# Cross attention: row sums by GpSimd, a scaled head output, and output products that accumulate over 14 heads

## The reference, cut to what matters

```python
q = (inputs_q @ Wq).reshape(b, sq, H, HD) * (1.0 / np.sqrt(HD))
k = (inputs_kv @ Wk).reshape(b, skv, H, HD)
v = (inputs_kv @ Wv).reshape(b, skv, H, HD)
scores = jnp.einsum('bqhd,bkhd->bhqk', q, k)
attn = jax.nn.softmax(scores, axis=-1)
ctx = jnp.einsum('bhqk,bkhd->bqhd', attn, v).reshape(b, sq, H * HD)
return ctx @ Wo
```

## Time and profile before

| | us |
|---|---|
| median of 3 runs | 1637.68 (1637.64 to 1637.73) |
| the profiled execution | 1636.64 |
| its span | 1634.4 |
| PE busy | 1607.9 |
| DVE busy | 1093.6 |
| ACT busy | 703.9 |
| POOL busy | 167.9 |

### The profile page before, as it was taken

One profiled execution on the slowest core, in us unless ns is written; L12 is line 12 of the kernel. 1 busy time (PEld: TensorE's weight loads), 2 busy tenths in 40 slices (PEclk: granted clock), 3 DMA queues, 4 the chain that ended last, 5 costly groups with the idle time before them and its releaser, 6 DMA issues.

```text
span 1634.4 us, 22632 instructions
## 1 busy us (share of the span) xinstructions
PE 1607.9 (98%) x8766; PEld 1258.1 (77%) x8766; DVE 1093.6 (67%) x1742; ACT 703.9 (43%) x941; POOL 167.9 (10%) x233
## 2 busy tenths in 40 slices
PE   9999999999999999999999999999999999999998
PEld 8887888888888888888888888887857757544544
DVE  4445787777778778777777779999583762633333
ACT  4334454454445454444444445655341361322221
POOL 0001000000100000010000001111100072011110
PEclk9999999999999999999999999999999999999999
DMA  7876655554565555465454454334320517489994
GB/s 238 228 228 188 161 134 158 151 145 122 172 163 142 149 142 154 118 185 142 113 139 126 133 136 123 93 102 135 137 92 39 206 52 304 183 255 418 421 425 174
DMA packets 125513, 282.93 MB, mean 173 GB/s; under 512 B 7712, under 2 KB 83680, under 8 KB 119264
## 3 DMA queue, kind: packets, MB, share of 16 engines
q1 hardware_dynamic: 103104, 200.75, 38.7%
q0 software_dynamic: 22304, 80.75, 16.4%
HBM read 206.99 MB, written 74.48 MB: 172 GB/s over the span
## 4 chain that ended last, share of the span: by engine, by line
PE 83%; DVE 8%; DMA 3%; issue 3%; ACT 2%; POOL 0%; SPq 0%; DVEq 0%; ACTq 0%; POOLq 0%
PE bank L478 19%; PE bank L41 19%; PE bank L448 17%; PE bank L500 6%; PE bank L2172 5%; PE bank L499 3%; PE bank L2211 2%; PE bank L1738 2%; PE bank L2197 2%; PE bank L1752 1%; PE bank L526 1%; DVE S L830 1%; PE bank L2201 1%; DVE e_parts L851 1%; PE bank L2157 1%
## 5 line engine op out<-in xcount | busy, mean ns | idle before, releaser
L478 PE MATMUL bank<-wv_parts,cT_hi 128*128 128x512 f32 x1024 | 333.7, 389 | 1.5 <-DMA wv_parts<-wv_dram 1.4
L478 PEld LDWEIGHTS bank<-wv_parts,cT_hi 128*128 128x128 f32 x1024 | 192.2, 188 | 41.8 <-DMA wv_parts<-wv_dram 1.8
L851 DVE TENSOR_TENSOR e_parts<-S,e_parts 128x1024 fp32r<-128x1024 f32 (+1 forms) x129 | 156.8, 1215 | 84.7 <-ACT e_parts L656 82.6
L448 PE MATMUL bank<-cT_hi,wk_hi 128*128 128x512 f32 x512 | 204.6, 400 | 0.0
L647 ACT ACTIVATE S<-S 128x1024 f32<-128x1024 f32 (+1 forms) x129 | 135.9, 1053 | 152.7 <-DVE S L830 152.2
L448 PE MATMUL bank<-cT_lo,wk_hi 128*128 128x512 f32 x512 | 199.8, 390 | 0.0
L448 PE MATMUL bank<-cT_hi,wk_lo 128*128 128x512 f32 x512 | 199.7, 390 | 0.0
L478 PE MATMUL bank<-wv_parts,cT_lo 128*128 128x512 f32 x512 | 199.3, 389 | 0.0
L656 ACT CAST e_parts<-S 128x1024 fp32r<-128x1024 f32 (+1 forms) x129 | 134.8, 1045 | 135.1 <-PE bank L500 128.9
L843 DVE TENSOR_TENSOR esum<-esum,S 128x512 f32<-128x512 f32 x210 | 145.0, 691 | 71.7 <-ACT S L647 68.1
L803 DVE TENSOR_TENSOR mx<-mx,S 128x512 f32<-128x512 f32 x222 | 152.9, 689 | 12.8 <-ACT S L641 9.0
(11 more groups left out here) (300 smaller groups left out, 2661.9 us busy)
## 6 DMA issues: line engine op xcount, KB each, us to landing
w<-in_w_moe SPq DMA_DIRECT2D x32, 2304.0 KB, 14.0
v_dram<-v_out SPq DMA_DIRECT2D x112, 512.0 KB, 4.9
v_back<-v_dram POOLq DMA_DIRECT2D x110, 512.0 KB
ctx_nat<-in_ctx SPq DMA_DIRECT2D x8, 1024.0 KB, 5.1
ctx_raw<-in_ctxT SPq DMA_DIRECT2D x7, 1024.0 KB, 8.5
v_dram<-v_back SPq DMA_DIRECT2D x14, 512.0 KB, 4.8
v_late<-v_dram POOLq DMA_DIRECT2D x14, 512.0 KB
wv_parts<-wv_dram POOLq DMA_DIRECT2D x6, 1024.0 KB, 8.3
```

Source lines behind the costliest of these rows:

```text
L448: t = e.matmul(banks[b][:], l, r, start=(c == 0 and m == 0), stop=(c == DT - 1 and m == 2))
L478: t = e.matmul(banks[b][:], l, r, start=(c == 0 and m == 0), stop=(c == DT - 1 and m == 2))
L851: e.tensor_tensor(lo, S[:, of_chunk(j, m), :], hi.bitcast(F32), ALU.subtract).then_inc(e_split, 1)
```

## The change

For heads 0 to 13 (SUMMED = 14) GpSimd adds the partial sums over partitions with an all-reduce (`add_sums`), VectorE inverts the 256 sums on all partitions (`invert_row`) and multiplies oT by them (`scale_o`), and the output products of these heads accumulate in PSUM banks 5 and 4 without leaving them; `add_heads` adds the two banks to x once. Heads 14 and 15 are finished as before. Since bank 4 is taken, the query projections use the value banks. finish_head moves to chunk 4 (NCH // 2), project_q to chunk 7, after the last scores, and the loads of wq and wo change their waits.

```diff
+        SUMMED = XH - 2
+        def q_bank(h):
+            return banks[FIRST_Q_BANK if h < 2 else V_BANKS[0] if h < LATE + 2 else V_BANKS[1]]
...
             def project_q(h):
-                if h >= 3:
-                    e.wait_ge(x_added, TT * (h - 2))
-                matmuls(e, banks[Q_BANK][:, 0:T], ...
+                if h >= 2:
+                    e.wait_ge(v_split, units(h - 2, NCH - 1)[0] if h < LATE + 2 else QUADS * KVT)
+                matmuls(e, q_bank(h)[:, 0:T], ...
...
             def project_k(h, j):
                 elif n:
                     e.wait_ge(v_split, QUADS * KVT)
+                    e.wait_ge(q_split, h + 1)
...
             def project_v(u):
+                if g and kt % NCH == 0:
+                    e.wait_ge(q_split, HPQ * (g - 1) + kt // NCH + 2)
...
             def weigh(h, j):
                 if j == 0 and h:
-                    e.wait_ge(sum_inverted, h)
+                    e.wait_ge(o_moved, h)
+                    if h > SUMMED:
+                        e.wait_ge(scaled, h)
...
             def finish_head(h):
                 e.wait_ge(o_moved, h + 1)
-                if h < XH - 1:
+                if h == SUMMED:
                     columns_of_sums(h, slice(0, P))
+                if h >= SUMMED:
+                    e.wait_ge(x_added, TT * (h - SUMMED + 1))
+                else:
+                    e.wait_ge(scaled, h + 1)
                 e.wait_ge(wqo_in, qo_value["wo", h])
-                if h:
-                    e.wait_ge(x_added, TT * h)
-                e.wait_ge(q_split, min(h + 3, XH))
                 for i in range(TT):
-                    t = e.matmul(banks[Y_BANKS[i]][:], ..., start=True, stop=True)
+                    t = e.matmul(banks[Y_BANKS[i]][:], ...,
+                                 start=(h == 0 or h >= SUMMED), stop=(h >= SUMMED - 1))
...
TensorE, heads 0 to 11 (in the late loop alike)
-                    if j == 0 and h and starts_quad(h):
-                        finish_head(h - 1)
                     for u in units(h, j):
                         project_v(u)
                     scores(h + 1, j)
-                    if j == 0 and h and not starts_quad(h):
+                    if j == NCH // 2 and h:
                         finish_head(h - 1)
-                    if j == NCH // 2:
+                    if j == NCH - 1:
                         project_q(h + 2)
...
VectorE
+            def invert_row(h):
+                e.wait_ge(sum_ready, h + 1)
+                own.done(e.reciprocal(mxr[:], mxr[:]))
+            def scale_o(h):
+                own.wait(e)
+                e.wait_ge(o_moved, h + 1)
+                e.tensor_tensor(oT[:], oT[:], mxr[:], ALU.mult).then_inc(scaled, 1)
+            def add_heads():
+                e.wait_ge(y_projected, SUMMED)
+                for i in range(TT):
+                    e.tensor_tensor(x[:, i, :], banks[Y_BANKS[i]][:], x[:, i, :], ALU.add).then_inc(x_added, 1)
...
heads 1 to 11: invert_sum(h - 1) in chunk 0 and add_head(h - 1) in chunk 1 go, and after the next shift
+                    if j == 2 and h:
+                        invert_row(h - 1)
+                    if j == 3 and h:
+                        scale_o(h - 1)
heads 12 to 14: the same two go, and after split_k(h + 1, j + 1)
+                    if j == 2:
+                        invert_row(h - 1)
+                        scale_o(h - 1)
+                    if j == 5 and h == XH - 2:
+                        add_heads()
...
GpSimd, in chunk 0 behind largest_score(h)
+            def add_sums(h):
+                e.wait_ge(sum_folded, h + 1)
+                e.wait_ge(max_ready, h + 2)
+                e.partition_all_reduce(mxr[:], esum_t[:], P, bass.bass_isa.ReduceOp.add).then_inc(sum_ready, 1)
...
SyncE
+ wo of head h - 1 is loaded in chunk 0 (after q_projected >= h + 2), wq of head h + 2 in chunk 5
+ (after y_projected >= h); before, both were loaded in turn in chunks 1 and 5
```

More of the change, by code:

```diff
@@ L393, in sync_cross @@
                     load_wk(1)
-            loads = 2
             for h in range(XH):
                 for j in range(NCH):
[L397 to L401, removed]
                     if j == 0:
@@ L405, in sync_cross @@
                             e.wait_ge(*v_spilled(KVT - 1))
-                            load_qo(loads)
-                            loads += 1
+                            load_qo(qo_order.index(("wq", 2)))
+                        elif h < XH - 1:
+                            e.wait_ge(q_projected, h + 2)
+                            load_qo(qo_order.index(("wo", h - 1)))
                         if not has_halves(h):
                             load_wk(h + 2)
[L410 to L413, removed]
+                    if j == 1 and h == XH - 1:
+                        e.wait_ge(y_projected, h)
+                        load_qo(qo_order.index(("wo", h)))
                     if j == NCH - 2 and has_halves(h):
@@ L417, in sync_cross @@
                         spill(u)
+                    if j == 5 and 0 < h < XH - 1:
+                        e.wait_ge(y_projected, h)
+                        load_qo(qo_order.index(("wq", h + 2) if h + 2 < XH else ("wo", h)))
                     if half_at(h, j) is not None:
@@ L429, in project_q @@
                     e.wait_ge(q_split, h)
-                if h >= 3:
-                    e.wait_ge(x_added, TT * (h - 2))
-                matmuls(e, banks[Q_BANK][:, 0:T], [(wq_raw[:, c, :], xT[:, c, :]) for c in range(DT)]).then_inc(q_projected, 1)
+                if h >= 2:
+                    e.wait_ge(v_split, units(h - 2, NCH - 1)[0] if h < LATE + 2 else QUADS * KVT)
+                matmuls(e, q_bank(h)[:, 0:T], [(wq_raw[:, c, :], xT[:, c, :]) for c in range(DT)]).then_inc(q_projected, 1)
             def project_k(h, j):
@@ L518, in finish_head @@
                 e.wait_ge(o_moved, h + 1)
-                if h < XH - 1:
+                if h == SUMMED:
                     columns_of_sums(h, slice(0, P))
+                if h >= SUMMED:
+                    e.wait_ge(x_added, TT * (h - SUMMED + 1))
+                else:
+                    e.wait_ge(scaled, h + 1)
                 e.wait_ge(wqo_in, qo_value["wo", h])
-                if h:
-                    e.wait_ge(x_added, TT * h)
-                e.wait_ge(q_split, min(h + 3, XH))
                 for i in range(TT):
-                    t = e.matmul(banks[Y_BANKS[i]][:], oT[:, i * P:(i + 1) * P], wqo_raw[:], start=True, stop=True)
+                    t = e.matmul(banks[Y_BANKS[i]][:], oT[:, i * P:(i + 1) * P], wqo_raw[:],
+                                 start=(h == 0 or h >= SUMMED), stop=(h >= SUMMED - 1))
                 t.then_inc(y_projected, 1)
@@ L570, in tensor_cross @@
                     scores(h + 1, j)
-                    if j == 0:
+                    if j == NCH // 2:
                         finish_head(h - 1)
-                    if j == NCH // 2 and h + 2 < XH:
+                    if j == NCH - 1 and h + 2 < XH:
                         project_q(h + 2)
@@ L607, in round_q @@
                     e.wait_ge(scored, NCH * h)
-                e.activation(q_hi[:], banks[Q_BANK][:, 0:T], ACT.Copy, scale=Q_SCALE).then_inc(q_rounded, 1)
+                e.activation(q_hi[:], q_bank(h)[:, 0:T], ACT.Copy, scale=Q_SCALE).then_inc(q_rounded, 1)
             def round_ctx(j):
@@ L775, in split_q @@
                 e.wait_ge(q_rounded, h + 1)
-                e.scalar_tensor_tensor(q_lo[:], banks[Q_BANK][:, 0:T], Q_SCALE, q_hi[:].bitcast(F32),
+                e.scalar_tensor_tensor(q_lo[:], q_bank(h)[:, 0:T], Q_SCALE, q_hi[:].bitcast(F32),
                                        ALU.mult, ALU.subtract).then_inc(q_split, 1)
@@ L870, in fold_sum @@
                 e.tensor_reduce(esum_t[:], esum[:].rearrange("p a t -> p t a"), AX.X, ALU.add).then_inc(sum_folded, 1)
+            def invert_row(h):
[5 more added lines that the diff above has]
+                e.tensor_tensor(oT[:], oT[:], mxr[:], ALU.mult).then_inc(scaled, 1)
             def invert_sum(h):
                 e.wait_ge(sum_ready, h + 1)
-                if h:
-                    e.wait_ge(x_added, TT * h)
-                e.reciprocal(small[:, 0:TT], banks[O_BANK][:, T:T + TT]).then_inc(sum_inverted, 1)
+                if h > SUMMED:
+                    e.wait_ge(x_added, TT * (h - SUMMED + 1))
+                e.reciprocal(small[:, 0:TT], banks[O_BANK][:, T:T + TT]).then_inc(scaled, 1)
+            def add_heads():
+                e.wait_ge(y_projected, SUMMED)
+                for i in range(TT):
+                    e.tensor_tensor(x[:, i, :], banks[Y_BANKS[i]][:], x[:, i, :], ALU.add).then_inc(x_added, 1)
             def add_tile(h, i):
                 e.wait_ge(y_projected, h + 1)
-                e.wait_ge(sum_inverted, h + 1)
+                e.wait_ge(scaled, h + 1)
                 e.scalar_tensor_tensor(x[:, i, :], banks[Y_BANKS[i]][:], small[:, i:i + 1], x[:, i, :],
@@ L976, in vector_cross @@
```

(4 more changed lines are left out.)

14 lines of the change are left out of this document (6 added, 8 removed).

## The result

The changed kernel takes 1647.66 us (median of 6), the kernel before 1637.66: a ratio of 1.0059 with a 95% interval of 1.0046 to 1.0072, so 10.0 us slower. The forecast was 1645.4 in a range of 1639.5 to 1650.

What follows compares the result with a forecast made beforehand. TensorE bounds the first twelve heads, TensorE and VectorE together the late ones. -6.3 + 2.3 + 3.0 + 4.2 + 6.0 - 1.5 = +7.7 us on 1636.64 gives 1644.3; with the median 1.04 higher, 1645.4, range 1639.5 to 1650.

Steps and rivals of the forecast that it cites:

- (a): TensorE in heads 0 to 13: 14 pairs of column matmuls go, 0.45 us each, -6.3 us.
- (b): project_q, 1.70 us, moves to the head's end: keeps step at the turnover, loses its cover in late heads.
- (c): Turnover: output products leave, TensorE waits for e_lo; ordinary heads +2.3 us, quad starts +3.0, late heads +4.2.
- The port lock: Quad starts: VectorE's shift and the all-reduce of the sums block each other, 0.48 us added to each wait.
- (d): Heads 12 to 14: reciprocal and product delay k_lo of chunk 4, 2.0 us each, +6.0; relief of today's waits -1.5.
- the two waits in the sum: Late heads: TensorE waits about 1.4 us for e_lo at the turnover and 2.0 us for k_lo of chunk 4.
- SyncE: Loads of wo and wq wait for other work but have more than 20 us until use; nothing added.
- The cheap reciprocal: Rival, chance 0.14: reciprocal 1.34 us shorter, -4.0 in late heads, and no lock, -1.0; +2.7, about 1640.4 us.
- The faster side: Rival, chance 0.08: only TensorE's work counts, e_lo 8.3 us after the weighing begins in a late head; 1628 us.
- The clock: Rival, chance 0.11 with the port: late pauses bring half-clock stretches, 1.7 us lost each; with three, 1648 to 1651 us.
- The port taken ahead of the shift in late heads: Rival, chance 0.11 with the clock: new all-reduce goes before the shift in late heads, 3 x 1.06 us; 1648 to 1651.

Runs made afterwards that it cites:

- e11: Kernel before without the column matmuls of heads 0 to 14, a constant replacing the inverse of their sums: 1634.05 us, ratio 0.998.
- e9: Kernel before with project_q of heads 14 and 15 in chunk 7 instead of chunk 4 of heads 12 and 13, wq and wo loads moved along: 1639.07 us.
- e3: Changed kernel with GpSimd's all-reduce of the sums one chunk later: 1650.05 us.
- e5: Changed kernel with the key projection of chunk 2 ahead of weigh(h, 0) in the late heads: 1648.25 us.
- e2: Changed kernel with the reciprocal of 256 columns replaced by a product with a constant: 1642.90 us.
- e6: Changed kernel with the load of wq one chunk later, in chunk 6: 1650.65 us.
- e1: The changed kernel again with no edit, profiled at full clock: 1647.06 us, ratio 1.006.
- e7: Changed kernel with value matmuls ahead of weigh(h, 0), three in ordinary heads and twelve at quad starts: 1656.09 us.

## Why the prediction was right

Its direction and its range held, and so did its mechanism in the late heads, where most of the loss lies; it was 2.3 us short. By the cycles, with the columns booked: late heads forecast +7.35, measured +7.06; quads +2.1 and +2.4; the nine ordinary heads -1.75 and +0.70. So all of the shortfall lies in ordinary heads. Step by step:

**(a) The columns, -6.3.** Right as a price of TensorE's work (13.21 to 12.78 at an ordinary turnover of e11). The sum could book it in all 14 heads only because it booked the waits from the shortened path as well; by itself it is worth 3.9.

**(b) The query projection.** That it keeps step at the turnover and loses its cover in a late head was right: e9 gives +1.1 and +1.2 for heads 12 and 13. The prediction did not give it a term; it sits in the late waits.

**(c) The lost cover.** Ordinary heads: 0.26 was forecast and 0.29 waited, so the wait was sized right. The query projection did keep step: weigh(h - 1, 7) loses 0.17 us behind it, TensorE is ready 0.21 later and e_lo is done 0.19 later (11.44 us into the cycle in place of 11.25), since ScalarE's rounding of chunk 0's values moves with TensorE. The weighing starts 0.10 behind e_lo, not 0.05. What the sum left out is the restart: the first two matmuls of a weighing that has waited start 0.31 apart in place of 0.22, and weigh(h, 0) to weigh(h, 1) takes 5.65 to 5.68 in place of 5.56. Wait and restart together are 0.13 more than forecast, 1.2 us in nine heads. This is the mis-sized term.

Quad starts: +1.05 net of the columns forecast, +1.06 and +1.33 measured. The port lock there was forecast at 0.48 and is 0.42 (two shifts 2.77 in place of 2.35). Whether the cycle pays for it is open, since e3 only moved it. The Trainium skill (SBUF — State Buffer, "SBUF: two separate sides") says that such a pair excludes each other for the whole of an operation; the 1.64 and 2.49 us of shift and additions beside an all-reduce agree, and show that the rule holds for an all-reduce too.

Late heads: 1.4 was forecast. In head 12 the last scores start at 993.06, so that TensorE was ready at 993.18, and the weighing starts at 994.57: 1.39.

**(d) VectorE in late heads.** The reciprocal from SBUF is 1.75 us, forecast 1.76; the late cycle 51.72, forecast 51.7; TensorE's wait for k_lo of chunk 4 1.73, forecast 2.0. That k_lo of chunk 3 would come 1.24 earlier stands in the prediction without a row; it came 1.10 earlier (24.50 us into the cycle in place of 25.60). Heads 12 to 14 came to +7.06, the forecast with their columns to 4.2 + 6.0 - 1.5 - 1.35 = +7.35. But the two waits in the sum are not two causes. e5 took the first away and the cycle stayed: what sets it is VectorE's work from the turnover to the last k_lo, plus the query projection behind it. Read so, e2 (1.44 for the reciprocal) and e9 (1.1 to 1.2 for the query) make 2.5 to 2.6, and 2.42 is what heads 12 and 13 lost. Head 14 has no query projection: e2 gives back 1.48 of its 2.22, and no experiment takes the other 0.7 apart (add_heads stands there).

**SyncE, "both loads have more than 20 us until their use", at nothing.** The load of wq has the time, but the prediction did not ask what it lands beside. In heads 2 and 5 it delays v by 0.35 and 0.57 us, in head 9 by 0.11; the cycles of heads 2 and 5 changed by +0.41 and +0.64, those of the other ordinary heads by -0.05 on average. e6 shows that the collision is the cause. The term was missing.

Together 1.2 for wait and restart and 1.0 for the load are 2.2 of the 2.4 us that the ordinary heads missed; the errors in quads (+0.3) and late heads (-0.3) cancel, which is luck.

**The rivals.** The cheap reciprocal: excluded by its row; e2 shows it would have been 4.2 us, as priced (-4.0). The faster side: e_lo 9.8 us into the late cycle, not 8.3. The clock: none in the 14 cycles of e1, but e7 had a stretch of 1.7 us in an unchanged late head, so single executions can carry it. It is not needed for the result: the differences of e1's cycles add up to 10.15 us without it, against 10.0 between the medians. The port taken ahead of the shift in late heads: it did not happen (the shift at 989.74 took 1.23). But the prediction added nothing at all for the lock there, and the next shift took 1.52; that cost nothing at the turnover, since VectorE still waited 0.24 for ScalarE behind it. e3 shows what a lock costs where there is no such pause, 1.0 to 1.1 each.

Open: why the load of v is issued later in heads 2, 5 and 9, what the lock costs a quad start, the 0.7 of head 14, and the 0.74 of head 2 in e3.

## What to carry to other kernels

Work taken off the busiest engine pays only in the stages in which it is the one that sets the end: in e11 the same 0.43 us were worth 0.22 to 0.53 in nine heads and 0.05 or less in five. Before moving a piece of work out of a turnover, ask which chain it was covering, and add up the other engine's work between two of its fixed points, not the single waits, which only move. A load that is early enough can still make its neighbour late: look at what else is issued in the same microsecond. And when an experiment moves an operation to take a collision away, check what it meets in its new place.

## What the runs showed of the hardware

A VectorE operation with two SBUF inputs and a GpSimd all-reduce hold each other up. The all-reduce of 256 columns takes 1.06 us alone and was recorded with 1.74 to 2.75 when it met one; the vector operations grew from 1.22 to 1.52, 1.64 and 2.12, and two additions from 1.41 to 2.49. In head 12 of e1 the all-reduce, recorded 0.14 us behind the shift, waited; in e3 the addition recorded 0.18 us ahead of the all-reduce was the one that grew, so 0.2 us between two records does not tell which is held. k_lo, with one input from PSUM, kept its 0.69 beside an all-reduce. A VectorE reciprocal of 256 columns costs 1.75 us from SBUF as from PSUM, a product with a constant 0.28. In e1 the first two matmuls of a weighing start 0.31 us apart behind a wait for e_lo and behind the query projection, where 0.22 and 0.12 us are usual. A stretch of 3.4 us at half clock came in e5 and in e7 behind 1.67 of 3.4 us busy, as at the earlier trace rows, and cost 1.6 and 1.7 us, while in e1 pauses of 1.2 and 1.7 us, 23 us apart, with the same 1.67 of 3.4 us busy around the second, brought none.
